# Prologue of a two-matrix FFN kernel: weights from two DMA queues, small loads off Pool, conversions shared out anew, one activation table set, another order of products

## What is computed

```python
base = einsum('btd,od->bto', x, W)
logits = einsum('btd,ed->bte', x, Wr) + 5.0 * one_hot(language_ids, E)
topw, topi = top_k(logits, 2)
gates = sum(one_hot(topi, E) * softmax(topw)[..., None], axis=-2)
h = einsum('btd,erd->bter', x, A)
cond = base + 2.0 * einsum('bter,bte,eor->bto', h, gates, B)
out = x + einsum('bsi,io->bso', cond, sign) * softplus(scale)
```

## Time and profile before

| | |
|---|---|
| median of 3 runs | 172.59 us (172.31 to 173.74) |
| span of the profiled execution | 170.2 us |
| TensorE busy | 161.6 us (95%) |
| VectorE busy | 96.8 us (57%) |
| ScalarE busy | 66.9 us (39%) |
| GpSimd busy | 56.2 us (33%) |
| chain that ended last | TensorE 81%, VectorE 7%, DMA 4%, SP's queue 3%, ScalarE 2% |

### The profile page before, as it was taken

One profiled execution on the slowest core, in us unless ns is written; L12 is line 12 of the kernel. 1 busy time (PEld: TensorE's weight loads), 2 busy tenths in 40 slices (PEclk: granted clock), 3 DMA queues, 4 the chain that ended last, 5 costly groups with the idle time before them and its releaser, 6 DMA issues.

```text
span 170.2 us, 3736 instructions
## 1 busy us (share of the span) xinstructions
PE 161.6 (95%) x1082; PEld 154.8 (91%) x1082; DVE 96.8 (57%) x421; ACT 66.9 (39%) x176; POOL 56.2 (33%) x53
## 2 busy tenths in 40 slices
PE   7999389999999999999999999999999999999993
PEld 5567168999999999999999999999999999999982
DVE  0269897655555555555555555555555555555450
ACT  3143446534444334444434334334334444444240
POOL 7865354532222222222233333333333333333000
PEclk9999999999999999999999999999999999999999
DMA  3599320423433333333333333333333333111113
GB/s 122 155 311 190 88 62 4 123 87 101 147 107 120 117 121 120 121 117 124 116 120 123 113 122 122 116 122 121 120 123 123 123 123 123 62 62 63 66 62 123
DMA packets 26087, 19.51 MB, mean 115 GB/s; under 512 B 3904, under 2 KB 21088, under 8 KB 26080
## 3 DMA queue, kind: packets, MB, share of 16 engines
q1 hardware_dynamic: 26016, 19.43, 37.2%
q0 software_dynamic: 64, 0.00, 0.0%
HBM read 11.03 MB, written 8.39 MB: 114 GB/s over the span
## 4 chain that ended last, share of the span: by engine, by line
PE 81%; DVE 7%; DMA 4%; SPq 3%; ACT 2%; issue 1%; POOL 1%; DVEq 0%
PE pair L587 66%; PE pair L604 13%; DMA sign_in<-in_L_ffn_sign 4%; PE p_ht L611 2%; SPq L241 2%; SPq L242 1%; DVE xt L425 1%; DVE m_full L466 1%; POOL wide_lo L312 1%; ACT wide_hi L358 1%; DVE wide_lo L470 1%; DVE sp L441 1%; DVE sign_hi L402 1%; DVE b_lo L458 0%; ACT xt_hi L341 0%
## 5 line engine op out<-in xcount | busy, mean ns | idle before, releaser
L302 POOL TENSOR_TENSOR xt_lo<-xt,xt_hi 128x512 fp32r<-128x512 f32 x32 | 41.2, 1286 | 96.1 <-ACT xt_hi L341 96.1
L587 PE MATMUL pair<-wide_hi,xt_hi 128*128 128x256 f32 (+2 forms) x260 | 63.1, 320 | 0.4 <-DVE wide_lo L470 0.3
L587 PE MATMUL pair<-wide_hi,xt_lo 128*128 128x256 f32 (+2 forms) x260 | 60.3, 310 | 0.0
L587 PE MATMUL pair<-wide_lo,xt_hi 128*128 128x256 f32 (+2 forms) x260 | 60.3, 309 | 0.0
L587 PEld LDWEIGHTS pair<-wide_hi,xt_hi 128*128 128x128 f32 x260 | 40.0, 189 | 1.3 <-issue 0.7
L587 PEld LDWEIGHTS pair<-wide_hi,xt_lo 128*128 128x128 f32 x260 | 40.3, 188 | 0.0
L587 PEld LDWEIGHTS pair<-wide_lo,xt_hi 128*128 128x128 f32 x260 | 40.2, 188 | 0.0
L381 ACT ACTIVATE y<-pair 128x256 f32<-128x256 f32 x31 | 11.9, 385 | 45.0 <-PE pair L604 45.0
L489 DVE TENSOR_TENSOR logits<-pair,bias 128x8 f32<-128x8 f32 x32 | 5.3, 166 | 37.0 <-PE pair L587 37.0
L425 DVE STREAM_TRANSPOSE xt<-x_in 128x512 f32<-128x512 f32 x32 | 22.8, 711 | 3.9 <-DVE top L497 3.4
L341 ACT ACTIVATE xt_hi<-xt 128x512 fp32r<-128x512 f32 x32 | 20.3, 633 | 3.0 <-DVE xt L425 3.0
(11 more groups left out here) (82 smaller groups left out, 140.6 us busy)
## 6 DMA issues: line engine op xcount, KB each, us to landing
x_in<-in_x SPq DMA_DIRECT2D x128, 64.0 KB, 1.9
out<-y SPq DMA_DIRECT2D x31, 256.0 KB, 2.1
w_in<-in_L_cond_W SPq DMA_DIRECT2D x4, 256.0 KB, 6.9
sign_in<-in_L_ffn_sign SPq DMA_DIRECT2D x4, 256.0 KB, 6.6
a_in<-in_L_cond_A SPq DMA_DIRECT2D x4, 64.0 KB, 4.5
b_in<-in_L_cond_B SPq DMA_DIRECT2D x1, 256.0 KB, 4.6
out<-y SPq DMA_DIRECT2D x2, 128.0 KB, 1.8
wr_in<-in_L_cond_Wr SPq DMA_DIRECT2D x4, 4.0 KB
```

Of the source, the lines that this page charges most:

```text
L302: nc.gpsimd.tensor_tensor(xt_lo[n][:, :, :].rearrange("p j (g b) -> p g j b", g=NQ), xt[n][:, :, :, :], xt_hi[n][:, :, :].bitcast(FP32).re ...
L587: last = nc.tensor.matmul(pair[n][bank][:, at0:at0 + hi - lo], l[:, k, :], w[:, k, lo:hi], start=(opens and k == 0 and l is xt_hi[n] and w ...
```

## The change

The signs are issued by ACT, ahead of an explicit load of one activation table set that holds copy, exp and ln. Scale goes to SP behind the second quarter of w, ids to SP behind B. VectorE clears ident, wr_in and eye. Of the four sign_hi VectorE makes the first, ACT the other three (a semaphore of its own for the first). On VectorE the w_lo are spread through the softplus chain, b_lo goes ahead of the heads, tile 1's transpose and the routing bias go behind m_full. On ACT b_hi goes ahead of the heads, and tile 1's high part behind those of m; on Pool tile 1's low part goes behind those of m. TensorE takes the same products in another order of groups.

```diff
@@ -239,7 +240,8 @@
 
             for j in range(OC):
                 sp_eng.dma_start(w_in[:, j, :], w_load[:, j, :]).then_inc(w_loaded[j], 16)
-                sp_eng.dma_start(sign_in[:, j, :], sign_load[:, j, :]).then_inc(sign_loaded[j], 16)
+                if j == 1:
+                    sp_eng.dma_start(scale_in[:, :], scale.partition_broadcast(P)).then_inc(scale_loaded, 16)
             load(0, 0, 0)
...
+            sp_eng.dma_start(ids_in[:, :], lang_ids.rearrange("(p a) -> p a", a=1)).then_inc(ids_loaded, 16)
@@ -274,11 +277,6 @@
 
         @block.gpsimd
         def _(pool):
-            pool.dma_start(scale_in[:, :], scale.partition_broadcast(P)).then_inc(scale_loaded, 16)
-            pool.dma_start(ids_in[:, :], lang_ids.rearrange("(p a) -> p a", a=1)).then_inc(ids_loaded, 16)
-            nc.gpsimd.memset(wr_in[:, :], 0.0).then_inc(wr_zeroed, 1)
-            nc.gpsimd.memset(ident[:, :], 0.0).then_inc(zeroed, 1)
-            nc.gpsimd.memset(eye[:, :, :], 0.0).then_inc(zeroed, 1)
@@ -291,7 +289,10 @@
                     .then_inc(eye_made, 1)
 
             for j in range(OC):
-                pool.wait_ge(sign_hi_made, j + 1)
+                if j == 0:
+                    pool.wait_ge(first_sign_hi_made, 1)
+                else:
+                    pool.wait_ge(sign_hi_made, j)
@@ -304,8 +305,7 @@
                                         xt_hi[n][:, :, :].bitcast(FP32).rearrange("p j (g b) -> p g j b", g=NQ),
                                         ALU.subtract).then_inc(xt_lo_made, 1)
 
-            for t in range(LEAD):
-                low_x(0, t, 0)
+            low_x(0, 0, 0)
...
 
+            for t in range(1, LEAD):
+                low_x(0, t, 0)
+
@@ -322,16 +325,24 @@
         @block.scalar
         def _(act):
 
+            for j in range(OC):
+                act.dma_start(sign_in[:, j, :], sign_load[:, j, :]).then_inc(sign_loaded[j], 16)
+
+            nc.scalar.preload_act_table_set("natural_log_exp_and_others")
             for j in range(OC):
                 act.wait_ge(w_loaded[j], 16)
                 nc.scalar.activation(w_hi[:, j, :, :, :],
                                      w_in[:, j, :].rearrange("p (i k a) -> p k i a", i=NQ, k=KC),
                                      ACT.Copy).then_inc(w_hi_made, 1)
-
-            act.wait_ge(neg_abs_made, 1)
-            nc.scalar.activation(exp_neg[:, :], sp[:, 1:2], ACT.Exp).then_inc(exp_neg_made, 1)
-            act.wait_ge(exp_neg_made, 1)
-            nc.scalar.activation(ln_one[:, :], exp_neg[:, :], ACT.Ln, bias=1.0).then_inc(ln_one_made, 1)
+                if j > 0:
+                    act.wait_ge(sign_loaded[j], 16)
+                    nc.scalar.activation(sign_hi[:, j, :], sign_in[:, j, :], ACT.Copy).then_inc(sign_hi_made, 1)
+                if j == 1:
+                    act.wait_ge(neg_abs_made, 1)
+                    nc.scalar.activation(exp_neg[:, :], sp[:, 1:2], ACT.Exp).then_inc(exp_neg_made, 1)
+                    act.wait_ge(exp_neg_made, 1)
+                    nc.scalar.activation(ln_one[:, :], exp_neg[:, :], ACT.Ln, bias=1.0).then_inc(ln_one_made, 1)
+
@@ -343,19 +354,20 @@
 
             high_x(0, 0, 0, first=True)
 
+            act.wait_ge(b_loaded, 16)
+            nc.scalar.activation(b_hi[:, :, :, :], b_in[:, :, :].rearrange("p e (j r) -> p j e r", j=OC),
+                                 ACT.Copy).then_inc(b_hi_made, 1)
             act.wait_ge(head_turned, 1)
...
-            act.wait_ge(b_loaded, 16)
-            nc.scalar.activation(b_hi[:, :, :, :], b_in[:, :, :].rearrange("p e (j r) -> p j e r", j=OC),
-                                 ACT.Copy).then_inc(b_hi_made, 1)
-            for t in range(1, LEAD):
-                high_x(0, t, 0, first=True)
...
+
+            for t in range(1, LEAD):
+                high_x(0, t, 0, first=True)
@@ -396,25 +408,16 @@
                 dve.wait_ge(vec_done, chain[0])
 
             nc.vector.memset(warm_words[:, :], 0.0).then_inc(warm_zeroed, 1)
-
-            for j in range(OC):
-                dve.wait_ge(sign_loaded[j], 16)
-                nc.vector.tensor_copy(sign_hi[:, j, :], sign_in[:, j, :]).then_inc(sign_hi_made, 1)
+            nc.vector.memset(ident[:, :], 0.0).then_inc(zeroed, 1)
+            nc.vector.memset(wr_in[:, :], 0.0).then_inc(wr_zeroed, 1)
+            nc.vector.memset(eye[:, :, :], 0.0).then_inc(zeroed, 1)
+
+            def low_w(j):
+
                 dve.wait_ge(w_hi_made, j + 1)
                 nc.vector.tensor_tensor(w_lo[:, j, :, :, :],
                                         w_in[:, j, :].rearrange("p (i k a) -> p k i a", i=NQ, k=KC),
                                         w_hi[:, j, :, :, :].bitcast(FP32), ALU.subtract).then_inc(w_lo_made, 1)
-
-            dve.wait_ge(scale_loaded, 16)
-            link(nc.vector.tensor_scalar(sp[:, 0:1], scale_in[:, :], -1.0, None, ALU.mult))
-            nc.vector.tensor_tensor(sp[:, 1:2], sp[:, 0:1], scale_in[:, :], ALU.min).then_inc(neg_abs_made, 1)
-
...
 
@@ -425,40 +428,48 @@
                 nc.vector.transpose(xt[n][:, :, :, :].rearrange("p g j b -> p (g j b)"),
                                     x_in[n][:, :, :].rearrange("p g c -> p (g c)")).then_inc(xt_made, 1)
 
-            turn_x(0, 0, 0, first=True)
-
-            dve.wait_ge(a_loaded, 16 * NQ)
-            nc.vector.transpose(at[:, :, :, :].rearrange("p g j b -> p (g j b)"),
-                                a_in[:, :, :].rearrange("p g c -> p (g c)")).then_inc(head_turned, 1)
+            dve.wait_ge(sign_loaded[0], 16)
+            nc.vector.tensor_copy(sign_hi[:, 0, :], sign_in[:, 0, :]).then_inc(first_sign_hi_made, 1)
+            low_w(0)
+
+            dve.wait_ge(scale_loaded, 16)
+            link(nc.vector.tensor_scalar(sp[:, 0:1], scale_in[:, :], -1.0, None, ALU.mult))
+            nc.vector.tensor_tensor(sp[:, 1:2], sp[:, 0:1], scale_in[:, :], ALU.min).then_inc(neg_abs_made, 1)
+            low_w(1)
+
             dve.wait_ge(exp_neg_made, 1)
             link(nc.vector.tensor_scalar(sp[:, 2:3], exp_neg[:, :], 1.0, None, ALU.add))
...
             link(nc.vector.tensor_scalar(sp[:, 4:5], sp[:, 3:4], 0.0, None, ALU.is_equal))
+            low_w(2)
             link(nc.vector.tensor_tensor(sp[:, 5:6], sp[:, 3:4], sp[:, 4:5], ALU.add))
             link(nc.vector.reciprocal(sp[:, 6:7], sp[:, 5:6]))
             dve.wait_ge(ln_one_made, 1)
             link(nc.vector.tensor_tensor(sp[:, 7:8], ln_one[:, :], sp[:, 4:5], ALU.add))
+            turn_x(0, 0, 0, first=True)
             link(nc.vector.tensor_tensor(sp[:, 8:9], sp[:, 7:8], sp[:, 6:7], ALU.mult))
             link(nc.vector.tensor_tensor(sp[:, 9:10], sp[:, 8:9], exp_neg[:, :], ALU.mult))
             link(nc.vector.scalar_tensor_tensor(sp[:, 10:11], scale_in[:, :], 0.0, sp[:, 9:10], ALU.max, ALU.add))
+            low_w(3)
             nc.vector.tensor_scalar(sp[:, 11:12], sp[:, 10:11], SCALING, None, ALU.mult).then_inc(softplus_made, 1)
             softplus = sp[:, 10:11]
+
+            dve.wait_ge(a_loaded, 16 * NQ)
...
 
+            dve.wait_ge(b_hi_made, 1)
+            nc.vector.tensor_tensor(b_lo[:, :, :, :], b_in[:, :, :].rearrange("p e (j r) -> p j e r", j=OC),
+                                    b_hi[:, :, :, :].bitcast(FP32), ALU.subtract).then_inc(b_lo_made, 1)
             dve.wait_ge(head_hi_made, 2)
...
-
-            dve.wait_ge(b_hi_made, 1)
-            nc.vector.tensor_tensor(b_lo[:, :, :, :], b_in[:, :, :].rearrange("p e (j r) -> p j e r", j=OC),
-                                    b_hi[:, :, :, :].bitcast(FP32), ALU.subtract).then_inc(b_lo_made, 1)
-            for t in range(1, LEAD):
-                turn_x(0, t, 0, first=True)
 
             dve.wait_ge(eye_made, KC)
@@ -470,6 +481,16 @@
+
+            for t in range(1, LEAD):
+                turn_x(0, t, 0, first=True)
+
+            dve.wait_ge(ids_loaded, 16)
+            dve.wait_ge(experts_numbered, 1)
...
@@ -548,20 +569,42 @@
 
 
             w_cols = lambda part, j, k: part[:, j, k, :, :].rearrange("p i a -> p (i a)")
-            for j in range(OC - 1):
+            def high_high(j):
+
                 pe.wait_ge(w_hi_made, j + 1)
-                pe.wait_ge(sign_hi_made, j + 1)
+                if j == 0:
+                    pe.wait_ge(first_sign_hi_made, 1)
+                else:
+                    pe.wait_ge(sign_hi_made, j)
                 for k in range(KC):
                     nc.tensor.matmul(p_m[k][:, :], w_cols(w_hi, j, k), sign_hi[:, j, :], start=(j == 0), stop=False,
...
+
+            def low_high(j):
+
                 pe.wait_ge(w_lo_made, j + 1)
...
+
+            def high_low(j):
+
                 pe.wait_ge(sign_lo_made, j + 1)
...
+
+            high_high(0)
+            low_high(0)
+            high_high(1)
+            high_low(0)
+            low_high(1)
+            high_high(2)
+            high_low(1)
+            low_high(2)
+            high_low(2)
+            pe.wait_ge(w_hi_made, OC)
+            pe.wait_ge(sign_hi_made, OC - 1)
```

13 lines of the change are left out of this document (7 added, 6 removed).

## The result

The changed kernel takes **170.18 us** (median of 4 runs, 169.39 to 170.49). The kernel before, run beside it, takes 172.56 (172.31 to 173.74), so the ratio is 0.985, with a 95% interval of 0.980 to 0.989. It is faster by 1.5%, 2.4 us; I had forecast 166.7 us with a range up to 168.9. The direction was right. The size was not: 2.4 us instead of 5.9.

The account below looks back on a forecast made before the run. TensorE was taken as the bound, so only an earlier loop start counts: tile 1 at 23.4 instead of 29.29, 5.9 us off. Span 170.2 becomes 164.3; with 2.4 outside it, 166.7 us, range 165.7 to 168.9.

Parts of the forecast that it names:

- main case: Loads: Pool's software queue makes the 4.5 to 6.2 us gap, which goes; 5.9 us off, 166.7 us, chance 0.58.
- rival A: Loads land no earlier, the gap belonging to the first loads; 4.2 us off, 168.4 us, chance 0.18.
- ACT's start: Prologue on ACT: four loads issued ahead of the table load cost 0 to 0.2 us, taken as 0.1.
- Rival C: ACT held by its own issues, products 1.5 us late: 168.2 us, chance 0.09; near no change or above, 0.04.
- Memsets on VectorE: Prologue: clearing eye takes at most 2.7 us, inside VectorE's wait for sign(0); cost 0.
- Order of products: TensorE's prologue: the same 60 products in another order of groups, worth 0 by itself.
- D: Nothing moves because something outside the prologue sets the time; 172.6 us, chance 0.02.
- pairs at 6.1, 7.4 and 8.7: Prologue loads: second to fourth pairs of w and sign arrive at those times in us, at 407 GB/s.
- Scale on SP: Prologue: scale on SP's queue may land as late as 8.6 us without delaying exp and w_hi(2); cost 0.
- VectorE behind the products: Before m_full: VectorE's list, with waits behind Pool, done at 15 to 16.2 us; later needs covered by 1.0 and 0.6.
- rival B: VectorE becomes the bound between 14 and 21 us through waits behind Pool; 1.2 us lost, 167.9 us, chance 0.09.
- One table set: ACT: two table loads of 1.28 us removed, ahead of ln and at tile 0's exp; worth 0 each.

Follow-up runs that it names:

- e2: The changed kernel with the scale and ids loads back on Pool; 168.86 us, 0.978 of the kernel before.
- e8: The changed kernel with TensorE's products of W and sign in the order of the kernel before; 170.11 us, 0.984.
- e1: The kernel before with only the scale and ids loads moved from Pool to SP; 172.34 us, 0.999.
- e4: The changed kernel with Pool's subtraction for tile 3 waiting until VectorE has made `second` for tile 0; 170.35 us, 0.985.
- e6: The changed kernel with the routing bias ahead of m_full instead of behind tile 1's transpose; 170.03 us, 0.984.
- e11: The changed kernel with one-tensor softplus links, Pool's tile 3 subtraction waiting for tile 0's h_gated, and scale and ids on Pool; 167.94 us, 0.972.
- e12: The changed kernel with scale issued on SP behind the fourth quarter of w instead of the second; 172.03 us, 0.996.
- e9: The changed kernel with five two-tensor softplus links on VectorE written with one tensor and a word per partition; 168.83 us, 0.978.
- e3: The changed kernel without the explicit activation table set, so three table loads again; 169.86 us, 0.981.
- e7: The changed kernel with Pool's subtraction for tile 3 waiting for tile 0's h_gated, the end of the chain; 169.28 us, 0.980.
- e5: The changed kernel with three w_lo ahead of the softplus again and ScalarE's exp and ln behind the conversions; 171.64 us, 0.993.

## Why the prediction was right in sign and wrong in size

The sum gave a span of 164.3; it is 167.6 in the profiled execution, 3.3 more. TensorE's trace says where. Third group 7.97 in the sum, 8.72 measured: 0.75. From there to the triples 6.63 instead of 28 x 0.227 = 6.36, and a wait of 0.50 for w_lo(3): 0.77. That makes the 1.53 at tile 1 (23.4 against 24.93). Between tile 1 and tile 2 5.39 instead of 3.59: 1.80. Together 3.3. In the median 0.8 is added, since the profiled execution is that much faster than the median one, and 0.6 is taken off, since the forecast's 2.4 outside the span held 0.6 too much: 166.7 + 3.3 + 0.8 - 0.6 = 170.2.

This says where TensorE stood, not what each cause costs. The 0.75 and the 0.50 are no separate prices: with the third group on time the triples would have waited for w_lo(3) all the longer. In e2 the third group is 0.38 later than in the changed kernel and the kernel is faster, and in e8 another order of groups leaves the time as it is. What set the time is the chain from w(2) over VectorE's list to h_gated: 9.84 + 8.07 + 12.32 = 30.23.

Steps that held:
- **The software queue made the gap** (main case against rival A): e1 shows it. But the changed kernel did not need the move of the small loads for it; e2 has them on Pool and no gap.
- **ACT's start**: four issues take 1.96, the table load ends at 4.01, the first product is at 5.55 where I had 5.43. Rival C fell. The first four products take 1.00 and not 1.63: TensorE is at the higher of its levels by then, which was my low end. It brought nothing, since the third group waits 1.07 for its load.
- **Memsets on VectorE**: the clearing of eye takes 1.76 us from 1.66 on, inside the wait for sign(0).
- **Order of products 0**: e8 shows it.
- **b_lo ahead of the heads**: b2 follows without a wait.
- **D** fell: the span moved by what tile 2 moved.

Steps that failed:
- **DMA, "pairs at 6.1, 7.4 and 8.7".** I took the 407 GB/s of 8 to 10 us for all that follows the first pair. Here the stretches up to 7.5 us run at 152 to 214 GB/s, and w(1), w(2) and w(3) land at 7.40, 9.81 and 11.06: 1.3, 2.4 and 2.4 late. I followed them only to TensorE, where the third group is 0.75 late. The one that counted is w(2), at the head of the chain. No run has it at 7.4, so the share of the miss that it makes has no price of its own. Rival A was half right so: it had the third group at 9.6, I had it at 7.97, and it starts at 8.72.
- **Scale on SP, "0 in both cases".** I asked only whether scale comes in time for exp. It does: it lands at 7.90 to 8.40 in those traces, and with exp and ln done ScalarE still waits for w(2) in the changed kernel (0.94), e4, e6 and e8. I did not ask what scale does to the quarter behind it on the queue. w(2) lands at 9.81 to 10.96 in the nine traces with scale ahead of it, at 9.63 and 9.74 with scale on Pool (e2, e11), and at 8.79 with scale behind w(3) (e12). Only e2 prices the place on the queue: 0.56 in the traces, 1.3 in the medians, one blocked link less included.
- **"VectorE behind the products", "15 to 16.2".** I had allowed for three waits behind Pool and then set most of them off against waits for loads. Both came, one behind the other: 1.89 until scale (w_hi(1) was made no earlier than that) and 1.14 until w_hi(2), then 1.25 and 1.02 for two links of 0.16. VectorE is through with the heads at 17.9, 1.7 past my worse end. That is rival B in mechanism; its price was 1.2. e9 shows the links' share, 1.05.
- **"One table set, 0 each".** I asked who waited for the load at tile 0 and found nobody. I didn't ask whom the load held back: Pool's second subtraction, through ScalarE. In the changed kernel the two stand back to back (26.92, 2.52 us) over tile 0's top_no and second. e3, with the load there, needs 0.6 less from m_full to the transpose.
- **The term that was missing.** The sum ended at tile 1. Tile 0's chain on VectorE (bias, b2's low part, three transposes, the top-2 operations) had to come forward by as much as TensorE did, and with bias and tile 1's transpose newly behind m_full it was longer than before, 12.32 for 10.64. From m_full to h_gated VectorE works 12.3 us without a pause, 4.14 of them in the four blocked operations (0.79, 1.25, 0.91, 1.19). Unblocked they take 0.15, 0.23, 0.17 and 0.29, so 3.3 us of this stretch are blocking. At tile 2 the late chain gave back 1.80 of the 4.36 us. e7 shows 0.9 of that from one of the four; e6 shows that the first two were mostly cover.

## What to carry to other kernels

When a change brings one engine's work forward, follow the sum until every chain that feeds it has been moved by as much, here one tile further, and ask of each instruction removed not only who waited for it but whom it kept away. Follow each load to every engine that queues behind it, too: here the one that counted was not the one that TensorE waited for. Several operations of a few elements on VectorE are cheap only while GpSimd doesn't subtract. The 128x1 links of two tensors weren't held when written with one tensor and a word per partition (e9), but `bias` and `second` are written so at 128x8 and were. Where the form doesn't help, the GpSimd work that is not urgent can wait for the end of the whole chain, not for its first link (e7 against e4). Small loads belong where they neither stop the first large ones nor come late for what queues behind them; here Pool's queue was the better place once the weights came from two queues.

## What the runs showed of the hardware

- **Which operations Pool holds back.** A 128x1 operation on two tensors takes 0.16 alone and 1.02 to 1.26 beside a subtraction; a 128x1 one on one tensor and a word per partition takes 0.21 beside it (e9). A cast of 128x2 takes 0.91 for 0.17, one of 128x8 0.79 for 0.15, `bias` at 128x8 1.25 for 0.23, `second` at 128x8 1.19 for 0.29, `gate` at 128x8 1.33 for 0.23, w_lo at 128x512 1.68 for 0.68. A reciprocal of 128x1 takes 0.16 beside a subtraction. The Trainium skill (SBUF — State Buffer, "SBUF: two separate sides") has the lock for operations with two SBUF inputs or in a two-port mode. What has two tensors agrees with it (the 128x1 operations, gate, w_lo), and so does the 0.21. The casts, `bias` and `second` have one tensor each; by the page they would have to be in such a mode, which no run here shows.
- **Pool's loads and one queue.** Two loads of 128 words cut one hardware queue's traffic to 41 GB/s for 1.5 us and stretch its issues to 1.01 and 2.04 us; without them 179 GB/s, and 0.44 at most for w, sign and scale (e1). With the weights on two queues they did not (160 GB/s, e2).
- **A load of a word per partition on SP** takes 0.42 us to issue behind w(1) and lands 6.4 us after its issue starts (5.2 in e1, 8.9 behind w(3) in e12). From 6.0 to 7.5 us 152 GB/s are moved with it there and 362 without (e12); the same order of loads had 192 in e9 and 234 in e5, and with both small loads on Pool it is 189 (e2) and 168 (e11), so the size of this cost varies and is not SP's alone.
- **Open:** why the second quarter of w lands at 6.9 at the earliest and 7.1 to 7.8 with two queues, whatever the small loads do, and why the third varies by 1.1 us among traces of the same order of loads. The two queues alone on the kernel before were not run.
